# A decoder layer with routed experts: other places for loads, gathers, row choices and additions

## What is computed

```python
x = _layernorm(x + _L0_attn_ref(x, ...))
x = _layernorm(x + _L0_xattn_ref(x, ctx_1024, ...))
# inside the third part
topv, topi = jax.lax.top_k(xt @ gate_w, 2)
probs = jax.nn.softmax(topv, axis=-1)
for e in range(8):
    h = jax.nn.silu(xt @ w1[e]) * (xt @ w3[e])
    out = out + w[:, e:e + 1] * (h @ w2[e])
```

## Time and profile before

| | us |
|---|---|
| median of 3 runs | 1466.82 |
| lowest, highest | 1466.47, 1468.64 |
| the profiled execution | 1465.96 |
| its span in the profile | 1464.3 |

### The profile page before, as it was taken

One profiled execution on the slowest core, in us unless ns is written; L12 is line 12 of the kernel. 1 busy time (PEld: TensorE's weight loads), 2 busy tenths in 40 slices (PEclk: granted clock), 3 DMA queues, 4 the chain that ended last, 5 costly groups with the idle time before them and its releaser, 6 DMA issues. The chain is left out here.

```text
span 1464.3 us, 24568 instructions
## 1 busy us (share of the span) xinstructions
PE 1324.5 (90%) x7943; PEld 715.8 (49%) x7943; DVE 1027.5 (70%) x1958; ACT 808.1 (55%) x1460; POOL 373.4 (25%) x610
## 2 busy tenths in 40 slices
PE   7988999999999999998688999998857999999965
PEld 4443444444444444443344555454434556666652
DVE  5847777777777777777568787878667556566646
ACT  5547666666666666665356565757523444555422
POOL 5402020202020202013456473645227000000042
PEclk9999999999999999999789999999878999999978
DMA  8327767676666666694643535335476646566751
GB/s 246 58 63 132 151 112 143 116 147 115 142 122 137 122 132 127 129 180 95 235 85 70 136 64 131 72 74 106 92 213 242 204 144 207 200 222 226 228 153 59
DMA packets 451836, 206.18 MB, mean 141 GB/s; under 512 B 401056, under 2 KB 415392, under 8 KB 451744
## 3 DMA queue, kind: packets, MB, share of 16 engines
q1 hardware_dynamic: 448608, 196.67, 56.9%
q0 software_dynamic: 2560, 8.39, 1.9%
q10 hardware_dynamic: 576, 0.00, 0.0%
HBM read 87.38 MB, written 16.45 MB: 71 GB/s over the span
## 5 line engine op out<-in xcount | busy, mean ns | idle before, releaser
L1453 DVE SCALAR_TENSOR_TENSOR X<-xa_SC,xa_rs,X 128x1024 f16<-128x1024 f32 x128 | 164.3, 1283 | 98.3 <-issue 97.6
L1276 ACT ACTIVATE X<-xa_SC,xa_rs 128x1024 f16<-128x1024 f32 x128 | 147.1, 1149 | 110.5 <-POOL xa_rs L1007 110.5
L1145 PE MATMUL xa_psS<-xa_KT,xa_QT 128*128 128x512 f16 x768 | 186.4, 379 | 6.0 <-DVE xa_mn L1485 4.6
L1157 PE MATMUL xa_psO<-wide,xa_V 128*128 128x512 f16 x768 | 173.8, 383 | 7.2 <-DMA wide<-X 6.9
L1007 POOL TENSOR_SCALAR xa_rs<-xa_rc,flag 128x1 f32<-128x1 f32 x128 | 33.9, 265 | 517.0 <-DVE xa_rc L1446 517.0
L1485 DVE CUSTOM_DVE_ANT_0 xa_SC<-xa_psS,maskb 128x1024 f32<-128x1024 f32 x128 | 155.0, 1211 | 4.5 <-PE xa_psS L1145 2.4
L1298 ACT ACTIVATE xa_SC<-xa_SC,xa_mn 128x1024 f32<-128x1024 f32 x128 | 145.4, 1136 | 13.4 <-DVE xa_mn L1485 13.3
L1936 PE MATMUL rmoe_psG<-rmoe_XGT,W 128*128 128x352 f16 (+6 forms) x768 | 112.9, 298 | 17.1 <-DVE zeros L2067 8.1
L1157 PEld LDWEIGHTS xa_psO<-wide,xa_V 128*128 128x128 f16 x768 | 74.5, 98 | 102.6 <-issue 17.5
L1936 PE MATMUL rmoe_psU<-rmoe_XGT,W 128*128 128x352 f16 (+6 forms) x768 | 112.7, 296 | 7.1 <-issue 7.0
L1145 PEld LDWEIGHTS xa_psS<-xa_KT,xa_QT 128*128 128x128 f16 x768 | 73.3, 98 | 90.7 <-DVE xa_mn L1485 9.4
(11 more groups left out here) (291 smaller groups left out, 2273.9 us busy)
## 6 DMA issues: line engine op xcount, KB each, us to landing
first<-in_L_ffn_w_dram SPq DMA_DIRECT2D x14, 2048.0 KB, 11.9
W2raw<-in_L_ffn_w_dram SPq DMA_DIRECT2D x8, 2048.0 KB, 9.1
expert_rows_dram<-zeros SPq DMA_DIRECT2D x10, 512.0 KB, 9.7
xa_WPraw<-in_L_xattn_Wq_dram SPq DMA_DIRECT2D x8, 512.0 KB, 11.1
xa_WOraw<-in_L_xattn_Wo_dram SPq DMA_DIRECT2D x8, 512.0 KB, 4.7
first<-in_L_ffn_wq_dram SPq DMA_DIRECT2D x4, 1024.0 KB, 8.0
first<-in_L_ffn_wo_dram SPq DMA_DIRECT2D x4, 1024.0 KB, 5.7
first<-in_L_ffn_w_dram SPq DMA_DIRECT2D x8, 512.0 KB, 6.8
```

Of the source, the lines that this page charges most:

```text
L1145: last = nc.tensor.matmul(psS[j % NSC][:, c:c + cw], QT[b][:, hq, g, t * P:(t + 1) * P], KT[b][:, hk, c:c + cw], start=(q == 0), stop=(q = ...
L1157: last = nc.tensor.matmul(psO[:, c:], V[b][:, hv, blk, :], PT[g % NPT][:, blk, hp, c:], start=(blk + q == 0), stop=(blk == NBLK - 1 and q ...
L1276: nc.scalar.activation(PN[j % NPN][:, 0:w // P, 0, :], by_block(SC[j % NSC], w), ACT.Identity, scale=rs[:, j % 4:j % 4 + 1]).then_inc(norm ...
L1453: nc.vector.scalar_tensor_tensor(out=PN[j % NPN][:, 0:w // P, 1, :], in0=by_block(SC[j % NSC], w), scalar=rs[:, j % 4:j % 4 + 1], in1=PN[j ...
```

## The change

- In the last half of self attention the first parts of jobs 0, 1, 2 go from j = 5, 6, 7 to j = 7, 8, 9, and the jobs are finished at j = 9, 10, 11, 12 and no longer at 8, 9, 10, 12.
- In place 0 the next expert's W1 and W3 are loaded in four DMAs of 1 MB, each issued when the one before has landed. ACT's later waits on that semaphore are counted up by 32 accordingly.
- In every place SP issues the transposes of the next rows ahead of the next W2 load, and no longer behind it. ACT waits for W2 behind the first silu of a place, no longer ahead of it.
- The choice matrices and their transposes are made in places 1 to 4, two tiles in each (DVE in steps f = 0 and 1, SP between the W2 load and the stores), and no longer in the last place.
- POOL issues the gathers of tile t only when those of tile t - 2 have landed.
- DVE's additions go apart: one instruction in each of steps 4 to 7 (tiles 0 and 1), tiles 2 and 3 behind the steps, tiles 4 to 6 behind the low half of output tile 0, tile 7 behind `finish_rows(0)`.

```diff
-    late_slots = {8: ([("wo", 0)], []), 9: ([("wo", 1)], []), 10: ([("wo", 2)], []), 12: ([("wo", 3)], [])}
-    parts_at = {5: 0, 6: 1, 7: 2}
+    late_slots = {9: ([("wo", 0)], []), 10: ([("wo", 1)], []), 11: ([("wo", 2)], []), 12: ([("wo", 3)], [])}
+    parts_at = {7: 0, 8: 1, 9: 2}
...
+        choose_at = {p: range(2 * p - 2, 2 * p) for p in range(1, 5)}
...
-                        sp.dma_start(W13raw[:, i, :, :], w[bass.ds(named[p], 1)].rearrange("o (k p) f -> p (o k) f", p=P)).then_inc(w13_in, 16)
+                        rows = w[bass.ds(named[p], 1)].rearrange("o (k p) f -> p (o k) f", p=P)
+                        if first:
+                            for k in range(0, DC, 2):
+                                wait_from(sp, w13_in, 16 * (2 * i + k // 2))
+                                sp.dma_start(W13raw[:, i, k:k + 2, :], rows[:, k:k + 2, :]).then_inc(w13_in, 16)
+                        else:
+                            sp.dma_start(W13raw[:, i, :, :], rows).then_inc(w13_in, 16)
...
                     load_rows(p + 1)
+                    turn_rows(p + 1)
                     sp.wait_ge(w2_done, FC * (p + 1))
                     sp.dma_start(W2raw[:], ...).then_inc(w2_in, 16)
-                    turn_rows(p + 1)
-                if last:
-                    for t in range(NT):
+                if p in choose_at:
+                    for t in choose_at[p]:
                         sp.wait_ge(chosen_done, t + 1)
...
             for t in range(NT):
+                if t >= 2:
+                    pool.wait_ge(gathered[t - 2], 32)
                 for k, dst in enumerate((Y1, Y2)):
...
             def step(p, first, last):
-                if first:
-                    act.wait_ge(arrived[1], 16)
-                else:
-                    act.wait_ge(w2_in, 16 * p)
-                wait_from(act, down_ready, TILES_BEFORE[p])
                 c = CAPS[p]
...
                     nc.scalar.activation(SG[f % 2][:, 0:c], psG[f % 2][:, 0:c], ACT.Silu).then_inc(silu_done, 1)
+                    if f == 0:
+                        if first:
+                            act.wait_ge(arrived[1], 16)
+                        else:
+                            act.wait_ge(w2_in, 16 * p)
+                        wait_from(act, down_ready, TILES_BEFORE[p])
...
-                    if last and f < NT // 2:
-                        if f == 0:
+                    if p in choose_at and f < len(choose_at[p]):
+                        if choose_at[p][f] == 0:
                             dve.wait_ge(scattered, 16 * 2 * NT)
...
                     if last and f >= FC // 2:
-                        for t in range(2 * f - FC, 2 * f - FC + 2):
-                            combine(t)
+                        combine(f // 2 - 2, f % 2)
+                if last:
+                    combine(2)
+                    combine(3)
...
-                        if r:
+                        if r == 0:
+                            for t in range(4, 7):
+                                combine(t)
+                        else:
                             finish_rows(r - 1)
...
             over_experts(dve, step)
+            combine(NT - 1)
```

More of the change, by code:

```diff
@@ L2020, in step @@
                 if not last:
-                    act.wait_ge(w13_in, 32 * (p + 1))
+                    act.wait_ge(w13_in, 32 * (p + 2))
                     w13_high(w13_pieces)
@@ L2050, in w13_low, with combine @@
                     nc.vector.tensor_tensor(dst[:, 1], src, dst[:, 0], ALU.subtract).then_inc(w13_done, 1)
-            def combine(t):
-                dve.wait_ge(gathered[t], 32)
-                nc.vector.scalar_tensor_tensor(out=X[:, t, :], in0=Y1[:, t, :], scalar=p12[:, 0, t:t + 1],
-                                               in1=X[:, t, :], op0=ALU.mult, op1=ALU.add).then_inc(combined, 1)
-                dve.wait_ge(combined, 2 * t + 1)
-                nc.vector.scalar_tensor_tensor(out=X[:, t, :], in0=Y2[:, t, :], scalar=p12[:, 1, t:t + 1],
-                                               in1=X[:, t, :], op0=ALU.mult, op1=ALU.add).then_inc(combined, 1)
+            def combine(t, ks=(0, 1)):
+                for k in (ks,) if isinstance(ks, int) else ks:
+                    dve.wait_ge(gathered[t], 32)
+                    wait_from(dve, combined, 2 * t + k)
+                    nc.vector.scalar_tensor_tensor(out=X[:, t, :], in0=(Y1, Y2)[k][:, t, :], scalar=p12[:, k, t:t + 1],
+                                                   in1=X[:, t, :], op0=ALU.mult, op1=ALU.add).then_inc(combined, 1)
             def step(p, first, last):
@@ L2079, in step @@
                                                 ALU.subtract).then_inc(h_lo, 1)
-                    if last and f < NT // 2:
-                        if f == 0:
+                    if p in choose_at and f < len(choose_at[p]):
+                        if choose_at[p][f] == 0:
                             dve.wait_ge(scattered, 16 * 2 * NT)
-                        for t in range(2 * f, 2 * f + 2):
-                            nc.vector.tensor_scalar(chosen[:, t, :], row1[:], last_at[:, t:t + 1], None,
-                                                    ALU.is_equal).then_inc(chosen_done, 1)
+                        t = choose_at[p][f]
+                        nc.vector.tensor_scalar(chosen[:, t, :], row1[:], last_at[:, t:t + 1], None,
+                                                ALU.is_equal).then_inc(chosen_done, 1)
                     if last and f >= FC // 2:
-                        for t in range(2 * f - FC, 2 * f - FC + 2):
-                            combine(t)
+                        combine(f // 2 - 2, f % 2)
+                if last:
+                    combine(2)
+                    combine(3)
                 for r in range(TILES[p]):
```

## The result

| | us |
|---|---|
| before, median of 5 runs beside the changed kernel | 1466.47 |
| after, median of 5 runs | 1454.17 (1451.33 to 1457.35) |
| ratio, with 95% interval | 0.9922 [0.9897, 0.9947] |
| profiled execution of after, its span | 1457.35, 1455.8 |

A forecast was written before the change was run, and what follows sets the result against it. PE was taken to set the pace almost everywhere, so only its pauses and lower clock pay: 4.0 + 3.6 + 0.3 + 18.3 = 26.2 off 1465.96 gives 1439.8, by the median 1440.6, predicted as 1441; range 1434 to 1456.

The forecast's parts named there:

- Part A: Last half of self attention: jobs two tiles later shrink PE's wait for the output weights; 4.0 us, ends 2.0 and 5.6.
- Part B: Place 0: first weights in four parts remove ACT's stop and put PE one step ahead; 3.6 us, ends 0 and 5.2.
- Part C: Transposes ahead of the W2 load: PE's wait ahead of place 7 goes, 2.5 us, plus 0.3 ahead of place 4.
- Parts D and E: Row choice in places 1 to 4, paced gathers: no transposes beside gathers; cost 0, pacing free.
- Part F: Place 7 and the end: PE without pauses at full clock, 20.8 us less; 18.3 after deductions of 1.5 and 1.0.
- that being a matter of load: Premise that ACT and PE stop where POOL's indirect DMAs and SP's DMAs run together because of the load.
- rival 2: Place 0 and place 7: the stops come from the gathers themselves; gain 6.3 us, time 1460.5, chance 0.14.
- The end: Behind the low half of output tile 1: all stays but tile 7's two additions, now inside, 1.5 us more.
- lower clock in steps 5 and 6: Place 7, up steps: 2.6 us of the 20.8 less, counted as won back from PE's lower clock.
- Rival 1: Place 0 or start of place 7: one stop of about 5 us stays; gain 17.5, time 1449, chance 0.22.
- Rival 3: Place 7: pacing makes the last gathers late and DVE waits 1 to 5 us; 1442 to 1446, chance 0.10.
- Rival 4: Places 1 to 4: the stops move there with the choice transposes; slower, 1477, chance 0.06.

The follow-up runs named there:

- two_loads: Changed kernel with place 0's first W1 and W3 loads again as two transfers of 2 MB; 1456.95 us, ratio 0.9924.
- after_again: The changed kernel run again without an edit; 1457.72 us, ratio 0.9925 to the kernel before.
- gathers_unpaced: Changed kernel with the 16 gathers issued back to back, without the pacing waits; 1459.07 us, ratio 0.9937.
- plain_loads: Changed kernel with 16 plain loads of consecutive rows, issued by SP, in place of POOL's gathers; 1442.62 us, ratio 0.9829.
- after_third: The changed kernel run once more without an edit, in a set without stops; 1439.97 us, ratio 0.994 beside a kernel before of 1448.75.
- choice_back: Changed kernel with the row choice and its transposes back in place 7; 1444.43 us, ratio 0.9954; run again as choice_back_2, 1440.35 us.
- before_again: The kernel before run again without an edit, in a set with stops; 1463.84 us, ratio 0.9992.
- set 2: Runs on one chip beside a kernel before of 1467.67 us, with stops; the changed kernel there takes 1457.72 us.
- jobs_and_turns: Kernel before with only the self attention jobs two tiles later and the row transposes ahead of the W2 load; 1460.33 us, ratio 0.9949.
- sets 1 and 3: Two groups of runs, each on one chip beside the kernel before: 1467.76 us in the first, 1449.72 us in the third.
- jobs_alone: Kernel before with only the jobs of self attention's last half two tiles later; 1466.32 us, ratio 0.9987.
- pair_by_pair_2: Changed kernel with each pair of gathers waiting for the landing of the pair just before, second run; 1455.58 us, ratio 1.0035.

## Why the prediction was wrong

**Part A, right.** Forecast 4.0, ends 2.0 and 5.6; 3.0 at tile 15 and 3.4 at place 0. The wait ahead of the output projection vanished, as allowed; the nine matmuls got 1.9 of their 2.0 us back. Not foreseen was that the value group moved ahead of the wait has a wait of its own, 4.33 us for transposes, and that the clock falls there instead.

**Part B, wrong.** Forecast 3.6, ends 0 and 5.2; measured 0.4 in the ledger, and two_loads shows no worth in it. ACT's stop did not go with the size of the loads: with small ones it is 5.56 (after), 3.67 and 4.32 us (after_again, gathers_unpaced), with large ones 5.23 in before and none in two_loads. The sentence "ACT did not stop in place 1 beside plain loads alone" was the evidence that failed: it tells that plain loads are harmless, which plain_loads confirmed, not that large ones make gathers harmful. DVE's long instruction stayed, as said, but step 5 and not 6 followed the pause, 6.33 us long. From the first matmul of place 0 to its down projection it is 40.3 us in after, 33.7 in after_third and 35.2 to 36.8 in the other kernels without stops; so 3.6 was a fair size for a place without the stop, and the condition that small loads bring it about was wrong.

**Part C, right.** 2.8 in all forecast, 2.9 measured between places 1 and 7; W2's later arrival cost nothing.

**Parts D and E, costs right, gain wrong.** Neither cost time, and neither took the stops away. gathers_unpaced, in a set with stops, equals the changed kernel. For part D both tests (choice_back and choice_back_2) fell into sets without stops, so whether it shortens them is not known: with the transposes in place 7 five profiles have 16.5 to 18.9 us of stops, without them four have 14.4 to 17.4.

**Part F, wrong where it mattered.** 17.3 us forecast inside place 7 without part C, 4.0 measured; with the end counted in, 15.8 and 1.7. The step that failed is the premise "that being a matter of load". The row that spoke against it was read and put under rival 2: between 1412 and 1416 only the gathers' queue had packets, and ACT stood. After has the same: from 1398 to 1407 all packets but one (of instructions) are of the gathers' queue, and ACT stands for 9.41 us; the stops sum to 17.4 us. The runs put the gathers themselves in the place of the load: 30.2 us and no stop with none or with plain loads of the same size at a higher share, in a set whose other kernels have stops.

What is sized right is the rest: with no stop, place 7 takes 30.20 us in 11 profiles, which is the forecast's 19.7 + 10.4, and the median of 1439.97 is 1 us from the 1441 predicted. But the kernel before is then at 1448.75, so the gain is 8.8 and not 26, and that the time comes near the forecast is luck: it belongs to a set of runs in which before doesn't stop either, and not to anything the change did to the stops.

Two smaller terms were off. The end cost 2.3 instead of 1.5: 1.8 from the second low half on (tile 7's two additions), 0.5 between the down projection and it. The 2.6 us put down to a lower clock in steps 5 and 6 are no gain by themselves either. The clock was low (0.50 from 1418 to 1424 in before), but in before_again PE gets through steps 5 and 6 in 5.9 us where before needs 7.5, and from the end of the last stop to the last low half of h it is 16.2 us in both: DVE with its four additions a step sets that time. By these rows only both terms together, the clock and the additions, could give the 3.6 us; that is an estimate. Of the 4.0 us that did come, 1.0 is in the down projection (11.5 to 10.5, the additions), and 3.0 in the up steps, where the stops are 1.0 shorter in sum and fall at other steps; what made up these 3.0 is not shown, since no kernel with the additions alone was run.

**Rivals.** Rival 2 named the mechanism and gave 6.3 us, 1460.5; the gain was 12.3 us (10.0 in set 2), and of what it lacked the additions explain 1.0 us in the down projection of the first pair, or 2.3 if after is set against jobs_and_turns. The prediction leaned on a page for it: the Trainium skill (Runtime: NRT & Kernel Launch, section Instruction fetch mechanics) has fetches mostly hidden. The trace agrees in so far as after and after_third show three and two packets in the instruction queues from 1386 to 1420, with and without 17 us of stops. That speaks against fetches as the cause, but not for any other. Rival 1 (one stop stays) is out, three did. Rival 3 (pacing holds, 1 to 5 us) did not come with `t - 2`; with `gathered[t - 1]` it costs 15.6 us. Rival 4 did not show: in after PE is busy 230.00 of the 230.00 us from 1155 to 1385, places 1 to 6.

**What stays open** is what makes a set stop. Shown is: in place 7 the stops need POOL's indirect DMAs (none with plain loads or no gathers), they hit ACT and PE's issue (DVE stands as well, but its rows only show it waiting behind ACT's silu), they are absent in two of the sets for the same program (sets 1 and 3 name the same chip, one with stops and one without), and where they are present the trace lacks the landing records of those DMAs. The last may mean that the recording of events takes part in it; that is a guess. The Trainium skill (NOTIFIC — Programmer's Manual, section When the ring fills) says that a full ring of event records, by the setting of its queue, loses the new record, overwrites the oldest or holds up the engine that produces it. Lost records and engines that stand are both in that list, though one setting gives only one of them. No run here shows such a ring, none was made without the recording, and which of the two, the stops or the missing records, brings the other is not known.

## What to carry to other kernels

Before costing an edit at the whole of a pause, ask what the pause waited for; where the profile names nothing, price the edit at what is left if the pause stays, and spend the first experiment on removing the suspected partner altogether (here the gathers, then plain loads in their place), since two runs settled here what parts B, D, E and F had assumed. Look at a second profile of the kernel before, from another set of runs: 16 to 19 us of it came and went with the set, more than the change was worth, so kernels of different sets must not be compared, and a gain needs the kernel before beside it. If gathers must run where ACT is on the path, starting them behind its last silu is worth 6.4 us where stops exist and costs up to 4.7 where they don't (there measured with a start at the sixth silu), so no version that was run beats the changed kernel in both.

## What the runs showed of the hardware

- Sixteen indirect gathers of 256 KB, issued by POOL about 1.3 us apart beside the up steps of place 7, go with 14 to 19 us of stops on ACT in three sets and the first pair of profiles, and with none in two sets, at the same DMA share (0.70 in after, 0.68 in after_third). Plain loads of the same 4 MB at a share of 0.82 (plain_loads): none, in a set with stops.
- The Trainium skill (SBUF — State Buffer, section Who interferes with whom) says of the memory's ports that PE and ACT never wait on anyone. Whether a port was at work no row here shows. What rows show is that ACT stood up to 15.43 us (jobs_alone) beside gathers, waiting for nothing named, so that sentence must not be read beyond the ports.
- A gather lands 3.7 to 3.8 us after its issue (after_third), and 6.3 for those that were issued beside the transposes of the row choice (choice_back, 1396 to 1400); with one pair in flight at a time, a pair takes 5.0 to 5.5 us (pair_by_pair_2).
- The stops cost clock as well: after PE had trickled and then stood 5.34 us, the granted clock of after is 0.50 from 1406 to 1416, the 1.2 GHz level, and 1.00 in after_third.
